# A three-layer graph network on Trainium2: one of 56 gathered columns is fetched row by row from SyncE and ScalarE

## The reference, cut to what matters

```python
def _sage_conv(x, src, dst, Wl, bl, Wr):
    agg = jax.ops.segment_max(x[src], dst, num_segments=x.shape[0])
    agg = jnp.where(jnp.isfinite(agg), agg, 0.0)
    return agg @ Wl + bl + x @ Wr

h = jnp.maximum(_layernorm(x, axis=-1), 0.0)          # x: 6250 x 128
h = leaky_relu(_sage_conv(h, src, dst, Wl1, bl1, Wr1), 0.01)   # 128 -> 256
h = leaky_relu(_sage_conv(h, src, dst, Wl2, bl2, Wr2), 0.01)   # 256 -> 256
h = leaky_relu(_sage_conv(h, src, dst, Wl3, bl3, Wr3), 0.01)   # 256 -> 128
return x + h
```

## Time and profile before

| | |
|---|---|
| median of 3 runs | 6152.48 us (6151.45 to 6153.09) |
| the profiled execution: its time | 6149.21 us |
| its span, first to last instruction | 6147.2 us |
| GpSimd busy | 75% |
| VectorE busy | 47% |
| TensorE busy, ScalarE busy | 11%, 4% |
| mean granted TensorE clock | 0.53 |

### The profile page before, as it was taken

How to read it: one execution, slowest core, us unless ns; L and a number is a source line. 1 busy time by engine, 2 the same in 40 slices (tenths; PEclk the granted TensorE clock), 3 DMA queues, 4 the chain that set the end, 5 groups by cost and what they waited for, 6 DMA issues and landing times.

```text
span 6147.2 us, 24451 instructions
## 1 busy us (share of the span) xinstructions
PE 685.4 (11%) x2214; PEld 394.3 (6%) x2214; DVE 2902.2 (47%) x3636; ACT 227.5 (4%) x663; POOL 4599.8 (75%) x4874
## 2 busy tenths in 40 slices
PE   0111111111100770000000000056000000000003
PEld 0000000000000430000000000044000000000002
DVE  4333333333333555555555555565555555555556
ACT  1000000000000110000000000011000000000001
POOL 6777777777777777777777777767777777777776
PEclk7555555555555655555555555565555555555556
DMA  4333333333333576666666666667666666666665
GB/s 139 106 109 106 107 107 106 107 107 105 109 104 106 183 234 209 210 210 211 208 211 211 209 210 211 210 213 244 211 211 208 209 211 209 211 208 211 210 208 177
DMA packets 434294, 1088.81 MB, mean 177 GB/s; under 512 B 100294, under 2 KB 152779, under 8 KB 434267
## 3 DMA queue, kind: packets, MB, share of 16 engines
q0 software_dynamic: 206976, 530.17, 30.6%
q1 hardware_dynamic: 204506, 539.02, 23.5%
q10 hardware_dynamic: 22784, 19.34, 1.0%
HBM read 555.06 MB, written 533.07 MB: 177 GB/s over the span
## 4 chain that ended last, share of the span: by engine, by line
POOL 49%; issue 16%; DMA 1%; POOLq 1%; DVE 0%; PE 0%
POOL ring L396 47%; POOL ring L423 2%; POOLq L393 0%; DMA ring<-features,stage 0%; POOLq L390 0%; DMA patch<-running_max_log,patch_row 0%; DMA ring<-running_max_log,end_row 0%; DMA running_max_log<-patch 0%; POOL patch L413 0%; PE banks L987 0%; POOLq L403 0%; POOLq L392 0%; DVE z_sum L841 0%; DMA features<-h_out 0%; DVE ring L731 0%
## 5 line engine op out<-in xcount | busy, mean ns | idle before, releaser
L396 POOL DMA_INDIRECT ring<-features,stage x4692 | 4436.4, 946 | 1456.0 <-issue 1411.4
L731 DVE TENSOR_TENSOR ring<-banks,ring 128x1024 f32<-128x1024 f32 (+1 forms) x1173 | 1226.6, 1046 | 3047.3 <-DMA ring<-features,stage 3030.1
L703 DVE TENSOR_TENSOR banks<-ring,banks 128x1024 f32<-128x1024 f32 (+1 forms) x1173 | 1231.9, 1050 | 37.5
L956 PE MATMUL banks<-ident,ring 128*128 128x128 f32 x20 | 5.0, 427 | 3762.1 <-DVEq L743 3762.1
L930 PE MATMUL banks<-dst_low,own 128*128 128x394 bf16 x200 | 96.0, 480 | 1466.6 <-DVE own L679 1466.6
L956 PEld LDWEIGHTS banks<-ident,ring 128*128 128x128 f32 x20 | 3.9, 222 | 3763.5 <-DVEq L743 3537.2
L914 PE MATMUL banks<-wr,h_turned 128*128 128x256 f32 (+1 forms) x490 | 201.9, 554 | 96.0 <-ACT h_turned L1048 96.0
L1092 ACT ACTIVATE agg<-zeros 128x512 f32<-128x512 f32 x75 | 47.3, 630 | 3944.1 <-PE banks L987 3944.0
L423 POOL DMA_INDIRECT ring<-running_max_log,end_row x147 | 141.5, 962 | 65.4 <-issue 43.9
L684 DVE COPY stage<-edges 128x8 int32 (+1 forms) x588 | 137.2, 233 | 84.8 <-DVE banks L703 25.8
L916 PE MATMUL banks<-b,ones 1*128 1x256 f32 (+1 forms) x294 | 138.8, 568 | 0.0
(11 more groups left out here) (112 smaller groups left out, 566.5 us busy)
## 6 DMA issues: line engine op xcount, KB each, us to landing
running_max_log<-ring SPq DMA_DIRECT2D x782, 512.0 KB, 3.3
running_max_log<-ring SPq DMA_DIRECT2D x391, 256.0 KB, 2.2
ring<-features,stage POOLq DMA_INDIRECT x4692, 2.8
h_in<-features ACTq DMA_DIRECT2D x98, 128.0 KB, 2.7
features<-h_out SPq DMA_DIRECT2D x48, 256.0 KB, 2.3
h_in<-features ACTq DMA_DIRECT2D x49, 64.0 KB, 1.8
out<-h_out SPq DMA_DIRECT2D x24, 128.0 KB, 2.5
ring<-running_max_log,end_row POOLq DMA_INDIRECT x147, 2.9
```

Of the source, the lines that this page charges most:

```text
L396: pool.indirect_dma_start(ring[:, c * w:(c + 1) * w], None, tables[l], bass.IndirectOffsetOnAxis(ap=stage[:, b, u:u + 1].bitcast(U32), axi ...
L703: dve.tensor_tensor(sum_ps[:, 0:CHAINS * w].rearrange("p (h f) -> p h f", h=CHAINS), group(g - 1).rearrange("p (h f) -> p h f", h=CHAINS), ...
L731: dve.tensor_tensor(group(g), sum_ps[:, 0:CHAINS * w], group(g), ALU.max).then_inc(turn, 1)
```

## The change

- In each full step GpSimd gathers 55 columns instead of 56: block 6 has 7 (`by_pool`).
- The 128 rows of the 56th column (the last of chain 3) are fetched one by one: 60 by SyncE, in ten pieces of 6 placed behind the ring's log stores of blocks 0 to 4, and 68 by ScalarE, in four pieces of 17 ahead of `keep_pair`. Each is a DMA of one row, 512 B or 1 KB, whose address is a byte offset in a register. A piece begins with one load of 6 or 17 registers from SBUF (`row_places`).
- Both wait until VectorE is in group 1 of the step (so that group 13 of the step before has been read), and until the last block of the step before is in the log. VectorE waits for the rows ahead of group 13.
- ScalarE's loops are cut so that each of the 27 full steps has a `fetch_rows`; a pair of `keep_pair` now follows each fetch, where the pairs followed one another before.
- At the start SyncE loads the row numbers of the 27 columns, 27 x 128 words of 4 B, a word to an element, into `row_list`, and VectorE multiplies them by the row's bytes, twice (`row_at` for 128 and for 256 features).

The diff, without declarations of semaphores and the branch for unsorted edges:

```diff
@@ -28,6 +29,8 @@
 VARS_AFTER = (4, 8, 6, 3)
 RECIPROCAL_AFTER = 4
 DMA = 16
+SYNC_ROWS, SYNC_AT_ONCE = 60, 6
+ACT_AT_ONCE = 17
 LOWEST = -3.4028234663852886e38
 TOP_EXPONENT = 0x7F000000
 SLOPE = 0.01
@@ -78,8 +81,18 @@
         return [b for b in range(BLOCKS) if width(b, last)]
 
 
+    ROWS_OF = [(0, SYNC_ROWS), (SYNC_ROWS, P - SYNC_ROWS)]
+    FETCHED = [DMA * count for _, count in ROWS_OF]
+    assert LAST <= RING_COLS - CHAINS and all(f * (STEPS - 1) < 1 << 16 for f in FETCHED)
+    assert SYNC_ROWS % SYNC_AT_ONCE == 0 and (P - SYNC_ROWS) % ACT_AT_ONCE == 0
+    assert SYNC_ROWS // SYNC_AT_ONCE <= GROUPS - 3
+
+    def by_pool(b, last):
+
+        return width(b, last) - (b == BLOCKS - 1 and not last)
+
     OPENING = [CHAINS if b == LATE_BLOCK else width(b, True) for b in range(BLOCKS)]
-    LANDED = [DMA * ((STEPS - 1) * BLOCK_COLS + OPENING[b]) for b in range(BLOCKS)]
+    LANDED = [DMA * ((STEPS - 1) * by_pool(b, False) + OPENING[b]) for b in range(BLOCKS)]
     STORES_OF = [width(b, False) // CHAINS for b in range(BLOCKS)]
     LOGGED = [DMA * ((STEPS - 1) * STORES_OF[b] + width(b, True) // CHAINS) for b in range(BLOCKS)]
 
@@ -128,6 +141,8 @@
         dst_high = sb("dst_high", [P, CHAINS, RUN + 3], BF16)
         not_below = sb("not_below", [P, CHAINS, 2 * P], BF16)
         stage = sb("stage", [P, BLOCKS, BLOCK_COLS], I32)
+        row_list = sb("row_list", [STEPS - 1, P], I32)
+        row_at = {w: sb(f"row_at_{w}", [STEPS - 1, P], I32) for w in widths}
         end_row = sb("end_row", [P, TILES], I32)
         wl_sb, wr_sb, b_sb = [], [], []
         for l, (k, n) in enumerate(shapes):
@@ -287,6 +304,29 @@
                      (next_first[0:P - 1, :], own_runs[1:P, :, 0]),
                      (next_first[P - 1:P, 0:CHAINS - 1], own_runs[0:1, 1:CHAINS, 0])]
             return pairs
+
+        def list_of(edges_src):
+
+            last_chain = (CHAINS - 1) * P * RUN + GROUPS - 1
+            return bass.AP(edges_src.tensor, last_chain, [[GROUPS, STEPS - 1], [RUN, P]])
+
+        def row_places(k, engine, i, at, count, w):
+
+            first = ROWS_OF[k][0] + at
+            _, places = nc.values_load_multi_w_load_instructions(
+                bass.at_runtime_partition(row_at[w][0:1, first:first + count], i), engines=[engine],
+                min_val=0, max_val=(nodes - 1) * w * 4,
+                skip_runtime_bounds_check_because="src numbers rows of the feature table")
+            return places
+
+        def table_row(l, w, place):
+
+            return tables[l].rearrange("n f -> (n f)").bitcast(U8)[bass.ds(place, 4 * w)].rearrange("(a b) -> a b", a=1)
+
+        def row_slot(k, r, w):
+
+            p = ROWS_OF[k][0] + r
+            return ring[p:p + 1, (RING_COLS - 1) * w:RING_COLS * w].bitcast(U8)
 
         block = ctx.enter_context(nc.Block())
 
@@ -391,7 +434,7 @@
                             if not first or l:
                                 pool.wait_ge(logged[b], i * (DMA * STORES_OF[b]) + LOGGED[b] * l)
                             pool.sem_inc(gathers_open, 1)
-                        for u in range(width(b, last)):
+                        for u in range(by_pool(b, last)):
                             c = b * BLOCK_COLS + u
                             pool.indirect_dma_start(
                                 ring[:, c * w:(c + 1) * w], None, tables[l],
@@ -635,6 +678,9 @@
             dve.scalar_tensor_tensor(out=patch_row[:, :], in0=lead_row[:, :], scalar=part[:, 1:2], in1=lead_early[:, :],
                                      op0=ALU.add, op1=ALU.mult).then_inc(prep_done, 1)
             dve.memset(restart_turns[:, :, 0], LOWEST).then_inc(prep_done, 1)
+            dve.wait_ge(list_loaded, DMA)
+            for w in widths:
+                dve.tensor_scalar(row_at[w][:, :], row_list[:, :], float(4 * w), None, ALU.mult).then_inc(rows_placed, 1)
             dve.wait_ge(prep_done, PREP)
             dve.tensor_copy(restart_ps, restart[:, 0:RING_COLS]).then_inc(restart_staged, 1)
 
@@ -721,12 +767,18 @@
                                 stage_block(i, b - 1, 1)
                             if last and g == groups - 1:
                                 keep_lead(1)
-                            dve.wait_ge(landed[b], i * (DMA * BLOCK_COLS) + (LANDED[b] * l + DMA * OPENING[b] if last else
-                                                                               LANDED[b] * l + DMA * BLOCK_COLS))
+                            each = DMA * by_pool(b, False)
+                            dve.wait_ge(landed[b], i * each + (LANDED[b] * l + DMA * OPENING[b] if last else
+                                                               LANDED[b] * l + each))
                         elif last and b == LATE_BLOCK:
                             dve.wait_ge(turn, carried + 2 * g + 1)
                             keep_lead(0)
                             dve.wait_ge(late_landed, DMA * CHAINS * (l + 1))
+                        elif g == GROUPS - 1:
+                            dve.wait_ge(act_rows_landed, FETCHED[1])
+                            dve.sem_inc(act_rows_landed, -FETCHED[1])
+                            dve.wait_ge(sync_rows_landed, FETCHED[0])
+                            dve.sem_inc(sync_rows_landed, -FETCHED[0])
                         dve.wait_ge(turn, carried + 2 * g + 1)
                         dve.tensor_tensor(group(g), sum_ps[:, 0:CHAINS * w], group(g), ALU.max).then_inc(turn, 1)
                         if g == 0:
@@ -1079,12 +1131,34 @@
                         keep_turned(j, p, p < loads)
                         keep_own(j, p)
 
+                def fetch_rows(i):
+
+                    act.wait_ge(group_scanned, i * BLOCKS + (FIRSTS * l + 1))
+                    if isinstance(i, int):
+                        act.wait_ge(rows_placed, len(widths))
+                        if l:
+                            act.wait_ge(logged[BLOCKS - 1], LOGGED[BLOCKS - 1] * l)
+                    else:
+                        act.wait_ge(logged[BLOCKS - 1], i * (DMA * STORES_OF[BLOCKS - 1]) + LOGGED[BLOCKS - 1] * l)
+                    for first in range(0, ROWS_OF[1][1], ACT_AT_ONCE):
+                        places = row_places(1, mybir.EngineType.Activation, i, first, ACT_AT_ONCE, w)
+                        for r, place in enumerate(places):
+                            act.dma_start(row_slot(1, first + r, w), table_row(l, w, place)
+                                          ).then_inc(act_rows_landed, DMA)
+
                 load(0, 0)
                 load(1, 1)
-                with act.Fori(0, PAIRS - 2) as j:
+                fetch_rows(0)
+                keep_pair(0, 2)
+                with act.Fori(1, PAIRS - 2) as j:
+                    fetch_rows(j)
                     keep_pair(j, 2)
+                with act.Fori(PAIRS - 2, PAIRS) as j:
+                    fetch_rows(j)
                 keep_pair(PAIRS - 2, PAIR_TILES[-1])
                 keep_pair(PAIRS - 1, 0)
+                with act.Fori(PAIRS, STEPS - 1) as j:
+                    fetch_rows(j)
 
                 for q in range(PAIRS):
                     b = q % 3
@@ -1121,10 +1195,31 @@
                 sp.dma_start(wl_sb[l][:, :, :], wl.rearrange("(c p) n -> p c n", p=P)).then_inc(weights_loaded, DMA)
                 sp.dma_start(b_sb[l][:, :], bl.rearrange("(a n) -> a n", a=1)).then_inc(weights_loaded, DMA)
             sp.wait_ge(const_done, CONSTS)
+            with nc.allow_non_contiguous_dma(reason="one word of each row to fetch"):
+                sp.dma_start(row_list[:, :], list_of(src)).then_inc(list_loaded, DMA)
             for w in widths:
                 sp.dma_start(logs[w][NO_EDGES:EARLY_ROWS, :], empty_row[:, 0:w]).then_inc(empty_stored, DMA)
 
             for l, (w, n) in enumerate(shapes):
+
+                def fetch_rows(i, g):
+
+                    first = g * SYNC_AT_ONCE
+                    if g == 0:
+                        if isinstance(i, int):
+                            sp.wait_ge(rows_placed, len(widths))
+                            if l == 0:
+                                sp.wait_ge(h0_stored, DMA * HEAD_STEPS)
+                            else:
+                                for b in range(STORES):
+                                    sp.wait_ge(h_stored[b], PER_OUT * l)
+                                sp.wait_ge(logged[BLOCKS - 1], LOGGED[BLOCKS - 1] * l)
+                        else:
+                            sp.wait_ge(logged[BLOCKS - 1], i * (DMA * STORES_OF[BLOCKS - 1]) + LOGGED[BLOCKS - 1] * l)
+                    places = row_places(0, mybir.EngineType.SP, i, first, SYNC_AT_ONCE, w)
+                    for r, place in enumerate(places):
+                        sp.dma_start(row_slot(0, first + r, w), table_row(l, w, place)
+                                     ).then_inc(sync_rows_landed, DMA)
 
                 def log_step(i, last):
                     for b in used_blocks(last):
@@ -1134,12 +1229,17 @@
```

(9 more changed lines are left out.)

8 lines of the change are left out of this document (7 added, 1 removed).

## The result

| | kernel before | changed kernel |
|---|---|---|
| median of the runs on one chip | 6152.78 us (6151.45 to 6154.44, 4 runs) | 6053.12 us (6052.94 to 6054.51, 4 runs) |
| span of the profiled execution | 6147.2 us | 6051.3 us |
| instructions in the trace | 24451 | 47687 |

The ratio is 0.9838, with a 95% interval of 0.9821 to 0.9855: 99.7 us faster. The forecast of 6051 was 2 us off. Later experiments ran on other chips of the same type. On one of those the same program is 13% slower than the kernel before, and variants of it on two more are 12 to 15% slower (29% with the registers loaded one by one); the last experiments are about that.

The account below looks back on a forecast made before the run. GpSimd's making of gathers, 1.25 us each, was taken as the bound. Removing 81 saves 101.2 us and all added work is hidden at 0: 6152.5 - 101.2 = 6051.3 us, range 6040 to 6400.

Parts of the forecast that it names:

- The bound: In the step loop, GpSimd's making of gathers sets the pace, 1.25 us each, not the moving of data.
- What is removed: One gather in each of 27 full steps of 3 layers, 81 x 1.25 = 101.2 us, all on the path.
- ScalarE's share: In each full step ScalarE's fetch, F, of 68 rows and 4 register loads takes 45 us, bounds 25 and 89: hidden.
- SyncE's share: In each full step SyncE's last rows land 52 us into the step and are needed at 61.5.
- ScalarE's pairs: After each fetch a pair takes 8.6 us, ending at 54 of 68.75 us; nothing waits for them at the end.
- DMA engines: Row packets add 6 to 11 us a step on each of 16 engines; share rises from 0.65 to at most 0.81.
- slower gathers: Rival: in the loop, added packets stretch GpSimd's 1.25 us a gather to 1.28, giving 6194 us; chance 0.04.
- The start: Before the first step, loading the list of 3456 words costs nothing, as 48 us of delay are free.
- the row fetch sets the step: Rival: late rows hold up VectorE's group 13 in each step, up to 98 us a step and 8420 us; chance 0.18.
- F + 8.7: Step time if rows are late and the next fetch waits for block 6's log: fetch F, 2.3 landing, 6.4 to log.
- the two queues share one generator: Milder form of the late-fetch rival: SyncE's 74 issues each hold ScalarE up 0.33 us; F = 69, 78 us a step, 6800 us.
- F + 8.6: Step time if rows are late and ScalarE's own loop closes: fetch F, then 8.6 us for the pair.

Follow-up runs that it names:

- e1: The changed kernel without the row fetch, the 56th column left out altogether: 6051.03 us, ratio 0.9836 to the kernel before.
- e9: The changed kernel with one gather of each full step covering 64 rows instead of 128, on another chip: 7867.55 us, ratio 1.1261 to the kernel before.
- e6: The changed kernel with each row transfer written as 16 equal parts, on another chip: 7846.94 us, ratio 1.1240 to the kernel before.
- e3: The changed kernel with 102 rows fetched by ScalarE instead of 68, and 26 by SyncE: 6454.26 us.
- e4: The changed kernel with 119 rows fetched by ScalarE instead of 68, and 9 by SyncE: 7065.23 us.
- e11: The changed kernel unaltered, on another chip where the kernel before takes 7000.56 us: 7941.62 us, ratio 1.1336.
- e2: The changed kernel with GpSimd gathering all 56 columns again and the rows also fetched, into an unread tile: 6153.92 us, ratio 1.0003 to the kernel before.

## Why the prediction was right, and where it was not

- **The bound** (GpSimd making gathers at 1.25 us each, whatever their bytes): right. Shown by e1 (101.2 us for 81 gathers), and by the half gathers of e9, which cost 3% less.
- **What is removed, 101.2 us**: measured 99.7 with the rows, 101.2 in e1 without.
- **ScalarE's share, F = 45**: measured 42.8. Both terms were a little off, to opposite sides: a row issue costs 0.38 us with its move, 25.8 for 68, where 28.6 was taken; the four loads cost 2.2 + 3 x 4.9 = 17.0, where 16.4 was taken. The load's price was right by luck: it was worked out per register, but the same 17 registers take 2.2 us ahead of the row issues and 4.9 behind them. Over the layers F is 38.2, 43.0 and 43.2 (medians), where the prediction had one value.
- **SyncE's share, 45.5 + 6.7 = 52 us into the step**: its last row is issued 2446.9 - 2394.8 = 52 us after group 0's maximum, so some 2 us later it has landed, where the prediction had it landed at 52. Group 13's maximum stands at 62.1. That leaves 8 us, where the prediction had 9.5 (52 against 61.5).
- **ScalarE's pairs**: hidden. They now follow a fetch each; the wait of 60.81 us ahead of `h_turned` is mostly the fetch, and nobody waits for its result.
- **DMA engines, a share of up to 0.81**: over-sized. It rested on "about 16 belong to a transfer whatever its size". ScalarE's queue has 33800 - 22784 = 11016 packets more for 5508 rows: two each, and as many when the row is written as 16 parts (e6). The share is 0.68. The sum had this term at nothing, so the time didn't suffer, but the weight given to slower gathers did.
- **The start, nothing**: right. In the changed kernel the list is issued at 31.38 and VectorE multiplies without a wait at 40.07 (its timeline):

```profile
40.07 0.21 DVE L683 TENSOR_SCALAR row_at<-row_list 27x128 int32<-27x128 int32 x1
```

- **Rival "the row fetch sets the step"**: not so on the first chip. Where e3 and e4 bring it about there, F + 8.7 holds to 0.3 us, but in the second layer it is the rival's other loop, ScalarE's fetch and pair, that sets when the next fetch begins. On the chip of e11 the rival came true, through SyncE and not ScalarE: a step of 90.2. The 0.18 it was given counted only unknown prices of instructions, not that the same instruction has another price on another chip. The forecast held on the chip that the result was taken on; on e11's it would have failed, and nothing in the working told the two apart. To that extent it was luck.
- **Rival "the two queues share one generator"**: the size was wrong, the mechanism can't be ruled out. ScalarE was to be held up by 24 us a step. Its 68 row issues of the second layer sum to 18.7 us (median) where 68 x 0.231 would be 15.7, so in the changed kernel it is held up by 3 us at most. SyncE's log store takes 0.38 us instead of 0.33 while rows are fetched, but also at 2450.68, when ScalarE's rows had been out for 11 us; and in e4 it takes 0.33 from 3102.96 on, with ScalarE's rows still going out and SyncE's done. So that 0.05 us goes with SyncE's own rows. In e3, where SyncE's log stores come in a burst, both queues' issues take 1 us and more. The Trainium skill (Perfetto Trace Analysis, DMA Instruction — HWDGE (DVE, Sync)) says the generator is locked for exclusive use; that burst agrees with it, and doesn't show that it is the lock.
- **Rival "slower gathers"**: 946 ns in e2 as in the kernel before, and 1.25 us from start to start. Landing went from 2.8 to 3.3 us and cost nothing.

## What to carry to other kernels

When one engine does nothing but issue, work moved to a queue that is idle is paid in full: 1.25 us a gather here, for 43 us of ScalarE's and 50 us of SyncE's otherwise mostly idle time in each step. Before doing it, write down the loop that closes if the moved work is late (here F + 8.6 by the pair, F + 8.7 by the log), since past its threshold the price isn't the excess of one step but that of all of them; and test the size by shifting work from one queue to the other. Look then at the trace for which loop closes: in e3 it was not the one that the total seemed to confirm. A kernel that hangs on the issue rate of queues should be timed on several chips: this one was 1.6% faster on one and 13% slower on another, and the tight medians of the first didn't hint at it.

## What was not expected of the hardware

- An indirect gather costs GpSimd 0.945 us and 0.30 of gap with 512 B rows as with 1 KB; with 64 rows instead of 128 it costs 0.90 and 0.30.
- A DMA of one row of 512 B or 1 KB takes 0.23 us to issue from ScalarE or SyncE, where a load of `h_in` takes 0.345 and a log store 0.33; with its register move a new row starts 0.32 us behind the last at the best and every 0.38 on ScalarE's average; with the loads shared out it is 42.8 / 68 = 0.63.
- A burst of log stores on SyncE's queue slows ScalarE's as well: in e3 a row issue then takes 1.02 us and a log store up to 1.38, where they take 0.23 and 0.33 otherwise.
- A load of registers from SBUF has no fixed price: 17 take 1.5 us at the least, and in the changed kernel's second layer 2.5 at the head of a fetch and 5.0 behind 17 row issues; one takes 0.46, on another chip.
- Chips of one type differ: the kernel before takes 6152 us on one and 6981 to 7001 on three others, and in the traces taken there single instructions of SyncE's and ScalarE's queues take 0.70 us where they take 0.03 to 0.33.
